# One core, metaformer layer: channel products over token tiles of 128 in place of 112, with the last 16 tokens in strips

## The reference, cut to what matters

```python
theta = cbr(x, th_w); phi = cbr(x, ph_w)          # first half: over pixels
Gs = einsum('bci,bcj->bij', theta, phi)
...
x = sigmoid(W_ys) * x                              # gated tokens: x1 in the kernel
xc = transpose(x.reshape(b, c, hw), (0, 2, 1))     # 784 tokens x 128 channels
theta_c = cbr(xc, thc_w)                           # 196 x 784 weights each
phi_c = cbr(xc, phc_w)
Gc = einsum('bcs,bsd->bcd', theta_c, phi_c)
g_xc = mean(cbr(xc, gxc_w), axis=1)
...
x = x + sigmoid(W_yc) * x1
t = t + experts(layer_norm(t))                     # second half: router, 8 experts, top 2
```

## Time and profile before

| what | us |
|---|---|
| median of three runs | 1913.96 |
| the profiled execution's own time | 1912.15 |
| its span, first to last instruction | 1910.1 |
| TensorE busy | 1834.2 (96%) |
| VectorE busy | 1505.3 (79%) |
| ScalarE busy | 1174.2 (61%) |
| GpSimd busy | 1128.1 (59%) |
| mean granted TensorE clock | 0.992 of full |

### The profile page before, as it was taken

How to read it: one execution, slowest core, us unless ns; L and a number is a source line. 1 busy time by engine, 2 the same in 40 slices (tenths; PEclk the granted TensorE clock), 3 DMA queues, 4 the chain that set the end, 5 groups by cost and what they waited for, 6 DMA issues and landing times.

```text
span 1910.1 us, 39142 instructions
## 1 busy us (share of the span) xinstructions
PE 1834.2 (96%) x13396; PEld 1342.4 (70%) x13396; DVE 1505.3 (79%) x4697; ACT 1174.2 (61%) x3240; POOL 1128.1 (59%) x1233
## 2 busy tenths in 40 slices
PE   4889999999999999999999999999999999999996
PEld 3567777777777777767777777777777777776774
DVE  5368878878888888887878888887888887887666
ACT  4446665656665666666665666565666566666544
POOL 2236556656556757556666655666655675755465
PEclk9899999999999999999999999999999999999998
DMA  4111212121222121222211122212121212121111
GB/s 130 51 69 61 77 69 86 69 80 49 77 69 86 69 86 52 76 70 77 82 73 66 63 77 69 86 69 74 55 77 69 86 69 86 52 69 60 44 52 51
DMA packets 43344, 135.10 MB, mean 71 GB/s; under 512 B 7980, under 2 KB 9597, under 8 KB 43150
## 3 DMA queue, kind: packets, MB, share of 16 engines
q1 hardware_dynamic: 42488, 130.78, 19.5%
q10 hardware_dynamic: 662, 1.84, 0.3%
HBM read 106.50 MB, written 26.10 MB: 69 GB/s over the span
## 4 chain that ended last, share of the span: by engine, by line
PE 61%; ACT 19%; DVE 8%; POOL 7%; issue 3%; DMA 1%; SPq 1%; ACTq 0%; POOLq 0%; DVEq 0%
ACT part L746 9%; PE rot L999 4%; PE rot L979 4%; PE rot L1043 4%; PE rot L1044 4%; PE rot L1053 4%; ACT j L618 4%; PE high L1188 4%; PE low L1188 3%; POOL x1l L517 3%; PE high L1189 3%; PE high L1190 3%; PE rot L1141 3%; PE rot L1179 3%; PE rot L915 3%
## 5 line engine op out<-in xcount | busy, mean ns | idle before, releaser
L1613 DVE SCALAR_TENSOR_TENSOR part<-high,gv,part 128x128 f32<-128x128 f32 (+1 forms) x1664 | 463.4, 341 | 129.1 <-ACT part L746 116.8
L746 ACT ACTIVATE part<-low,gv 128x128 f32<-128x128 f32 (+1 forms) x1664 | 467.8, 375 | 142.1 <-POOL otok L530 73.0
L525 POOL TENSOR_TENSOR part<-part 128x256 f32<-128x256 f32 (+1 forms) x416 | 341.3, 820 | 283.3 <-DVE part L1613 279.4
L530 POOL TENSOR_TENSOR otok<-part 128x128 f32<-128x128 f32 (+1 forms) x416 | 281.7, 677 | 32.6
L1043 PE MATMUL rot<-x1h,wch 112*128 112x256 f32 x1120 | 278.1, 286 | 0.7 <-ACT chan L693 0.7
L1044 PE MATMUL rot<-x1h,wcl 112*128 112x256 f32 x1120 | 272.5, 281 | 0.0
L500 POOL TENSOR_TENSOR tp_l<-tp,tp_h 128x448 fp32r<-128x448 f32 x64 | 71.8, 1122 | 268.5 <-ACT tp_h L632 268.5
L1043 PEld LDWEIGHTS rot<-x1h,wch 112*128 112x128 f32 x1120 | 212.1, 189 | 6.1 <-issue 1.1
L1044 PEld LDWEIGHTS rot<-x1h,wcl 112*128 112x128 f32 x1120 | 212.6, 190 | 1.4
L1188 PE MATMUL low<-weh,xh 128*128 128x512 f32 (+1 forms) x416 | 180.2, 433 | 6.3 <-ACT part L746 5.1
L517 POOL TENSOR_TENSOR x1l<-tok,x1h 112x1024 fp32r<-112x1024 f32 x64 | 136.0, 2126 | 84.5 <-ACT x1h L686 84.5
(11 more groups left out here) (225 smaller groups left out, 3754.3 us busy)
## 6 DMA issues: line engine op xcount, KB each, us to landing
xin<-in_x SPq DMA_DIRECT2D x32, 784.0 KB, 4.3
y_ch<-rstd_rows SPq DMA_DIRECT2D x32, 784.0 KB, 4.0
x<-in_x SPq DMA_DIRECT2D x32, 784.0 KB, 4.3
cen<-shift_rows SPq DMA_DIRECT2D x32, 784.0 KB, 4.1
out<-x SPq DMA_DIRECT2D x64, 392.0 KB, 2.4
otok<-in_ggs_w SPq DMA_DIRECT2D x1, 600.2 KB
tok<-in_ggs_w SPq DMA_DIRECT2D x1, 600.2 KB
rstd_rows<-both_rows SPq DMA_DIRECT2D x32, 6.1 KB
```

Of the source, the lines that this page charges most:

```text
L525: nc.gpsimd.tensor_tensor(part[0:n, slot, 0:2, :], part[0:n, slot, 0:2, :], part[0:n, slot, 2:4, :], ALU.add).then_inc(sem("half_sum"), 1)
L530: nc.gpsimd.tensor_tensor(otok[0:n, i, :], part[0:n, slot, 0, :], part[0:n, slot, 1, :], ALU.add).then_inc(sem("token_ready"), 1)
L746: last = nc.scalar.activation(part[0:n, turn % RING, e, :], low[turn % 2][0:n, e * C:(e + 1) * C], ACT.Copy, scale=gv[par(p, back)][0:n, i ...
L1613: last = nc.vector.scalar_tensor_tensor(out=own, in0=high[turn % 2][0:n, e * C:(e + 1) * C], scalar=gv[par(p, back)][0:n, i, HALF + e:HALF ...
```

## The change

Tokens are cut into tiles of 128: six whole tiles (`WHOLE` = 6) and a seventh that starts at token 656 (`REST`), so that only its last 16 tokens, on partitions 112 to 127, are new. For the seventh tile the three products (high x high, low x high, high x low) become one matmul: the operands `x1h[:, 6]` and `wrest` carry them in strips of 32 partitions. A per-partition factor `valid` makes the weights of the tokens that tile six already had zero. This takes one instruction for the whole tiles and three small casts on ScalarE for group 1, and one small subtraction behind the shorter one on GpSimd. The matmuls of a block go from 21 to 19. Bodies of `to_tokens`, `to_channels`, the residual, the space gate and the row of 1/std follow the new cut; the row comes back in two transfers, one of 768 and one of 16 values for each image. The list of calls on each engine stays. The words that came with the change also speak of the large weights' transfers; the list `big` on ScalarE's queue and the lists on SyncE's queue stand in the same place in both programs, and the diff has no line on them.

```diff
+WHOLE = S // 128
+REST = S - 128
...
-        wch = sb("wch", [T, NT, MT * 128], F32R)
-        wcl = sb("wcl", [T, NT, MT * 128], F32R)
+        wch = sb("wch", [128, WHOLE, MT * 128], F32R)
+        wcl = sb("wcl", [128, WHOLE, MT * 128], F32R)
+        wrest = sb("wrest", [128, MT * 128], F32R)
+        valid = sb("valid", [128, 1])
...
+        def cut(q):
+
+            return slice(512 * q, min(512 * q + 512, S))
...
+        def tokens(v, j):
+
+            if j < WHOLE:
+                return v[:, 128 * j:128 * j + 128]
+            return v[:, REST:S]
...
-                        row_in("rstd", y_ch[:, :, :].rearrange("p b s -> p (b s)"), back)
+                        sp.wait_ge(sem("rstd_row_out"), 16 * (turn(back) + 1))
+                        line = rows_dram["rstd"][turn(back) % 2].rearrange("(b j) t -> b (j t)", b=PAIR)
+                        full = 128 * WHOLE
+                        sp.dma_start(y_ch[:, :, 0:full], line[:, 0:full].partition_broadcast(128))\
+                          .then_inc(sem("rstd_spread"), 16)
+                        sp.dma_start(y_ch[:, :, full:S], line[:, 2 * full - REST:full + 128].partition_broadcast(128))\
+                          .then_inc(sem("rstd_spread"), 16)
...
                         need(pool, "x1_hi_ready", k, p, g + 1, back)
-                        nc.gpsimd.tensor_tensor(x1l[:, lo:hi, :, :], tok[third(k, p, back)][:, lo:hi, :, :],
-                                                x1h[:, lo:hi, :, :].bitcast(F32), ALU.subtract)\
-                            .then_inc(sem("x1_lo_ready"), 1)
+                        last = nc.gpsimd.tensor_tensor(x1l[:, lo:min(hi, WHOLE), :, :], own[:, lo:min(hi, WHOLE), :, :],
+                                                       x1h[:, lo:min(hi, WHOLE), :, :].bitcast(F32), ALU.subtract)
+                        if hi > WHOLE:
+                            last.then_inc(sem("x1_full_ready"), 1)
+                            need(pool, "x1_full_ready", k, p, 1, back)
+                            last = nc.gpsimd.tensor_tensor(x1h[96:128, WHOLE, :, :], own[96:128, WHOLE, :, :],
+                                                           x1h[96:128, WHOLE, :, :].bitcast(F32), ALU.subtract)
+                        last.then_inc(sem("x1_lo_ready"), 1)
+                        if hi > WHOLE:
+                            need(pool, "x1_lo_ready", k, p, 2, back)
...
                         need(act, "x1_ready", k, p, g + 1, back)
-                        nc.scalar.copy(x1h[:, lo:hi, :, :], tok[third(k, p, back)][:, lo:hi, :, :]).then_inc(sem("x1_hi_ready"), 1)
+                        last = nc.scalar.copy(x1h[:, lo:min(hi, WHOLE), :, :], own[:, lo:min(hi, WHOLE), :, :])
+                        if hi > WHOLE:
+                            nc.scalar.copy(x1h[64:128, WHOLE, :, :], own[64:128, WHOLE, :, :])
+                            for r in (0, 32):
+                                last = nc.scalar.copy(x1h[r:r + 32, WHOLE, :, :], own[96:128, WHOLE, :, :])
+                        last.then_inc(sem("x1_hi_ready"), 1)
...
-                                                   src[:, j, b, :], ident[0:T, 0:T])
...
+                    dst = bank(use, k, p, back)
+                    if q == 1:
+                        nc.tensor.transpose(dst[:, S - 544:S - 512], src[96:128, WHOLE, b, :], ident[96:128, 96:128])
+                    for j in range(QUART[q][0], min(QUART[q][1], WHOLE)):
+                        last = nc.tensor.transpose(dst[:, (j - QUART[q][0]) * 128:][:, 0:128], src[:, j, b, :], ident[:, :])
...
-                            lo = min(2 * g, NT - 2) * T
-                            last = nc.tensor.matmul(bank("slogit", k, p, back)[32 * g:32 * g + 32, 0:2 * T], wws2[:, :],
-                                                    hid[:, lo:lo + 2 * T], start=True, stop=True)
+                            lo = min(256 * g, S - 256)
+                            last = nc.tensor.matmul(bank("slogit", k, p, back)[32 * g:32 * g + 32, 0:256], wws2[:, :],
+                                                    hid[:, lo:lo + 256], start=True, stop=True)
...
-                        for j in range(lo, hi):
+                        for j in range(lo, min(hi, WHOLE)):
                             hi_x = x1h[:, j, :, :].rearrange("p b c -> p (b c)")
...
-                            last = nc.tensor.matmul(dst, wch[:, j, rows], x1l[:, j, :, :].rearrange("p b c -> p (b c)"),
-                                                    start=False, stop=(j == NT - 1))
-                    return last
+                            nc.tensor.matmul(dst, wch[:, j, rows], x1l[:, j, :, :].rearrange("p b c -> p (b c)"),
+                                             start=False, stop=False)
+                    return nc.tensor.matmul(dst, wrest[:, rows], x1h[:, WHOLE, :, :].rearrange("p b c -> p (b c)"),
+                                            start=False, stop=True)
```

More of the change, by code:

```diff
@@ L160, in metaformer_kernel @@
         xl = [sb(f"xl{p}", [C, PAIR, S], F32R) for p in range(2)]
-        st1 = sb("st1", [T, 2 * NT, 6])
+        st1 = sb("st1", [128, 2 * NT, 6])
         st2 = sb("st2", [128, TILES, 6])
         sm = sb("sm", [128, 5, 2 * NT])
-        tok = [sb(f"tok{r}", [T, NT, PAIR, C]) for r in range(3)]
-        mean1 = [sb(f"mean1_{p}", [T, 2 * NT]) for p in range(2)]
-        var1 = sb("var1", [T, 2 * NT])
-        rstd1 = [sb(f"rstd1_{p}", [T, 2 * NT]) for p in range(2)]
+        tok = [sb(f"tok{r}", [128, NT, PAIR, C]) for r in range(3)]
+        mean1 = [sb(f"mean1_{p}", [128, 2 * NT]) for p in range(2)]
+        var1 = sb("var1", [128, 2 * NT])
+        rstd1 = [sb(f"rstd1_{p}", [128, 2 * NT]) for p in range(2)]
         mean2 = sb("mean2", [128, TILES])
@@ L184, in metaformer_kernel @@
         hid = sb("hid", [128, S])
-        sl = sb("sl", [128, 2 * T])
-        sz = sb("sz", [T, 2 * NT])
-        se = sb("se", [T, 2 * NT])
-        sp1 = sb("sp1", [T, 2 * NT])
-        gain = sb("gain", [T, 2 * NT])
-        x1h = sb("x1h", [T, NT, PAIR, C], F32R)
-        x1l = sb("x1l", [T, NT, PAIR, C], F32R)
+        sl = sb("sl", [128, 256])
+        sz = sb("sz", [128, 2 * NT])
+        se = sb("se", [128, 2 * NT])
+        sp1 = sb("sp1", [128, 2 * NT])
+        gain = sb("gain", [128, 2 * NT])
+        x1h = sb("x1h", [128, NT, PAIR, C], F32R)
+        x1l = sb("x1l", [128, WHOLE, PAIR, C], F32R)
         chan = sb("chan", [128, MT, PAIR, C])
@@ L300, in metaformer_kernel @@
         raw_sws1 = scrap[0:DS, 3:4]
-        raw_sbs = scrap[0:T, 4:6]
+        raw_sbs = scrap[:, 4:6]
         raw_sc = scrap[:, 6:6 + MT]
@@ L515, in x1_low @@
                         lo, hi = QUART[g]
+                        own = tok[third(k, p, back)]
                         need(pool, "x1_hi_ready", k, p, g + 1, back)
-                        nc.gpsimd.tensor_tensor(x1l[:, lo:hi, :, :], tok[third(k, p, back)][:, lo:hi, :, :],
-                                                x1h[:, lo:hi, :, :].bitcast(F32), ALU.subtract)\
-                            .then_inc(sem("x1_lo_ready"), 1)
+                        last = nc.gpsimd.tensor_tensor(x1l[:, lo:min(hi, WHOLE), :, :], own[:, lo:min(hi, WHOLE), :, :],
[8 more added lines that the diff above has]
+                            need(pool, "x1_lo_ready", k, p, 2, back)
                 def add_token(i, back):
@@ L1030, in space_turn @@
                         for t in range(2):
-                            last = nc.tensor.transpose(bank("sturn", k, p, back)[0:T, 128 * t:128 * t + 128],
-                                                       sl[:, t * T:(t + 1) * T], ident[:, :])
+                            last = nc.tensor.transpose(bank("sturn", k, p, back)[:, 128 * t:128 * t + 128],
+                                                       sl[:, 128 * t:128 * t + 128], ident[:, :])
                         last.then_inc(sem("sturn_filled"), 1)
@@ L1519, in residual @@
                         need(dve, "x1_ch_filled", k, p, 2 * b + q + 1, back)
-                        nc.vector.scalar_tensor_tensor(out=x2[o][:, b, cols(q)], in0=bank(f"x1_ch{b}{q}", k, p, back)[:, 0:width(q)],
-                                                       scalar=cg[:, b:b + 1], in1=x2[o][:, b, cols(q)],
+                        nc.vector.scalar_tensor_tensor(out=x2[o][:, b, cut(q)], in0=bank(f"x1_ch{b}{q}", k, p, back)[:, 0:cut(q).stop - cut(q).start],
+                                                       scalar=cg[:, b:b + 1], in1=x2[o][:, b, cut(q)],
                                                        op0=ALU.mult, op1=ALU.add).then_inc(sem("x2_ready"), 1)
```

81 lines of the change are left out of this document (44 added, 37 removed).

## The result

The changed kernel takes 1973.02 us, the median of four runs (1967.5 to 1974.15), against 1915.66 for the kernel before in four (1911.57 to 1919.2). The ratio is 1.0292, with a 95% interval of 1.0273 to 1.031: slower, as forecast, but by 57 us where 22 were forecast, and 8 us above the range.

What follows compares the result with a forecast made beforehand. The chain of waits alternates between ScalarE with GpSimd, TensorE, VectorE's router and TensorE; only changes on it count. 1.11 - 0.47 + 0 + 0.12 = 0.76 us a step over 29 steps, +22 us: 1936 us, range 1910 to 1965.

Steps and rivals of the forecast that it cites:

- A: Stretch from `gx(0)` to `mixed`, chain on ScalarE and GpSimd: to grow by 1.11 us a step (1.05 to 1.66).
- GpSimd's share of A: Split subtraction on GpSimd ahead of its sums: 2.25 us instead of 1.85, so 0.40 more (0.34 to 0.65).
- B: Stretch from `mixed` to `finish(3)`, TensorE alone: to get 0.47 us a step shorter, at least 0.
- The transfers: The row's second transfer, in pieces of 64 B: hidden behind 3.8 us of cover, at no cost.
- blocks 2 and 3 (four, 0.47 us) are in B and count in full: Four matmuls taken off TensorE between `mixed` and `finish(3)`: the whole 0.47 us a step comes off.
- C: Stretch from `finish(3)` over the router on VectorE to `low_half(2)`: no change, block 4's two matmuls count nothing.
- The four take 0.62 + 3 x 0.41 - 3 x 0.10: ScalarE's four casts before `mixed`, overlapping by 0.10 us: 1.55 us, 0.71 more than the one cast; 1.01 more without overlap.
- Two tiny ones cost 0.05 us more, at most 0.17: Transposes of `x1_channels` on TensorE: twelve of 128 columns and two tiny ones cost 0.05 us more than fourteen of 112.
- D: Stretch from `low_half(2)` to the next `gx(0)`, on TensorE: 0.12 us a step longer (0 to 0.25).
- a second wait: Rival: later `x1l` causes a 0.5 us stall in B, on top of the high ends; 1969 us, chance 0.05.
- TensorE as the bound: Rival: waits at `mixed` are noise and ten matmuls in 32 steps come off, 37 us; 1877 us, chance 0.13.
- Cheap strips: Rival: 32-partition operations cost a fraction and casts overlap more, A grows 0.35 us; 0 a step, 1914 us, chance 0.18.

Runs made afterwards that it cites:

- b_drop4: The kernel before without four matmuls a step (low part of the tokens, tiles 4 and 5, blocks 2 and 3): 1913.73 us beside 1916.44.
- a_fullcasts: The changed kernel with the three small ScalarE casts made over all 128 partitions, 256 columns each: 1961.22 us.
- a_onecast: The changed kernel with the last tokens put into all strips by TensorE earlier, so one ScalarE cast replaces four: 1943.28 us.
- a_nosmall: The changed kernel without the two small transposes a step that bring the last tokens back to channels: 1954.36 us.
- c_dve_strip: The changed kernel with one cast, two `xl` after the router's gates, whole transposes for small ones, and the strip's subtraction on VectorE: 1886.79 us.
- b_late_xl: The kernel before with GpSimd's last two `xl` subtractions of a step made to wait for the router's gates: 1906.23 us.

## Why the prediction was right or wrong

**Right.** The direction, and for the reason given: the chain in A is ScalarE's and GpSimd's, so the matmuls taken from blocks 0 and 1 only make TensorE wait longer. It waits 43.4/30 + 16.6/29 = 2.0 us a step at `mixed` and inside block 0. That this is the forecast's number is in part luck: A grew by 0.26 us more than forecast, but TensorE's own work in A fell by 0.25 (16.97 to 16.72 us busy) and not by 0.47. GpSimd's share of A, 0.34 measured against 0.40 with ends of 0.34 and 0.65. B by itself, 0.58 shorter against 0.47. The transfers, hidden. The widened transposes, free. The forecast of the two sides of a step as such ("gets nothing for what it takes from the other side") held, and held in one stretch more than I applied it to.

**The step that failed first: "blocks 2 and 3 (four, 0.47 us) are in B and count in full", together with C at 0.** They count nothing (b_drop4), since B + C was a tie between TensorE's own matmuls and GpSimd's run from `x1l` to `xl`, at whose end the router's `eq` was held. The chain showed `eq` at 2.07 us beside operations of 0.27; I took C as the router's because the chain said VectorE, and did not ask why one operation of 104 columns needs 2 us. B's -0.47 and C's 0 came out as -0.58 and +0.60: 0.49 a step, 14 us.

The rule that would have warned me stands in the Trainium skill, SBUF — State Buffer, Summary: beside each other, of a VectorE operation with two SBUF inputs and a GpSimd one that reads SBUF, "the second one to issue **fully blocks** until the first finishes". The trace agrees and goes further: `eq` was blocked not for one instruction of GpSimd (1.0 us each) but until the last of those queued had ended, 2.65 us. I had weighed the contention for the strip's subtraction alone, where it made no difference: 0.76 us, not 1.05.

**"The four take 0.62 + 3 x 0.41 - 3 x 0.10".** The size of each was right, the overlap was not: casts whose first partition changes do not overlap (1.87 us), casts on the same partitions do (a_fullcasts). The prediction named 1.01 as the other end and chose 0.71 by "the row of overlap is one of the same kind"; it was not, in the one respect in which the new casts were new. 0.31 a step, 9 us. a_onecast puts the whole cost of the split casts at 24 us in full steps, 30 in the total.

**"Two tiny ones cost 0.05 us more, at most 0.17".** The two cost 0.51 us (a_nosmall). I priced them by their columns, and that was right only for the wide ones. 0.36 a step, 10 us. With `space_logit` (0.57 in the chain) D is +0.48, outside the 0 to 0.25 that I gave it.

Together, 14 + 9 + 10 less 2 for GpSimd's 0.06 is 31 of the 35 us missed; the rest is in the first and last steps, where the forecast had set two estimates against each other, at nothing. **The rivals:** a second wait, priced at 1969, came nearest in time, with the right culprit (VectorE against GpSimd) in the wrong stretch: the wait is in C, and it hides what B gave. That its number is so near is luck, since neither its A of 1.66 nor its D of 0.25 came. TensorE as the bound is refuted by b_drop4 and by every wait in A; it becomes true only in c_dve_strip, when casts, strip and `xl` are out of the way. Cheap strips are refuted on both engines: 32 partitions cost what 128 do for the same columns (0.40 and 0.76 us).

## What to carry to other kernels

An operation on the chain that takes several times as long as its equals may not be its engine's to shorten: look at what the other engines end at the same moment, and take that for the bound until a run says otherwise, before any work ahead of it is counted as a gain. Where two sides of a step arrive together, one side's savings are worth little and each side's additions count, so taking an operation away and adding one are not priced by the same row. Splitting one instruction into strips cost a whole instruction for each strip here, whatever its number of partitions; prepare the layout earlier, where an engine has time, and keep the late instruction in one piece.

## What the runs showed that I had not expected

- A VectorE comparison of 104 columns (0.26 us alone) takes up to 2.67 us beside four GpSimd subtractions and ends 0.12 to 0.13 us behind the last. The other way round, a GpSimd sum of 0.5 us takes 3.1 beside three VectorE operations with both inputs in SBUF and ends 0.33 us behind the last. An operation of VectorE with one input in PSUM and a reduction, just ahead of it and beside the same `xl`, took their usual 0.26 us.
- Neighbouring casts of 256 columns on ScalarE start 0.31 us apart (the same 128 partitions) or 0.41 apart (64, 32 and 32 partitions, each from another first partition).
- A lone 32 x 32 transpose costs TensorE 0.17 us, and 0.15 more on its neighbours where it stands among large ones; a 128 x 128 one costs 0.11 (0.66 for six).
- GpSimd takes 0.75 us for 256 columns on 32 partitions and 0.77 for a sum of 256 columns on 128.
- With the repairs the same products over tiles of 128 are 1.5% faster than the kernel before, where the change as it stands is 2.9% slower. Of the 1.5%, 0.5% come from `xl` behind the router, which the kernel before can have as well (b_late_xl).
